# Reordering the loads and set-up between the layer passes and the spectral mixing of a Fourier tokenizer kernel

## Chip, cores, metric

One core of one Trainium2 chip (trn2) runs the whole program once. The metric is the device time of that execution in microseconds (us). TensorE, VectorE, ScalarE, GpSimd and SyncE are called PE, DVE, ACT, POOL and SP, as in the profile. SP issues all the DMA transfers.

## What is computed

128 images of 64 x 64 x 3 go through a tokenizer of four Fourier layers with 32 channels, then through a small head (three dense layers), and the 64 x 64 result of each image is the token input of a transformer block (scan, attention, experts). The change lies in the tokenizer alone:

```python
h = layer_norm(x @ fc0_w + fc0_b, ln0_g, ln0_b)
for i in range(4):
    x1 = spectral_conv(h, w1[i], w2[i])   # rfft2, mix channels on 12 + 12 x 12 modes, irfft2
    x2 = einsum('bchw,oc->bohw', h, conv_w[i]) + conv_b[i]
    h = layer_norm(x1 + x2, ln_g[i], ln_b[i])
    if i < 3: h = gelu(h)
h = gelu(h @ fc1_w + fc1_b); h = gelu(h @ fc2_w + fc2_b); h = h @ fc3_w + fc3_b
```

## The kernel before

**Passes and mixings.** The images are worked in 64 pairs. A pass runs over all pairs, two per loop turn (`halves` = 32 turns); the parity of a pair is p, and most buffers are doubled by p. The first pass lifts the pixels and normalizes them; for each pair it stores the activation (`act_scratch`, 1024 KB, st_a) and its forward spectrum (`spectrum_in`, two DMAs of 78 KB, st_x). A mixing follows: for each of 12 ky it loads the spectrum of all images (`x_in`, 832 KB) and a block of weights (`w_raw`, 208 KB), multiplies them, and stores the result (`spectrum_out`, 832 KB, y_out). The next pass loads for each pair the activation (`act_in`) and the mixed spectrum (`z_in`, two DMAs), adds the pointwise convolution and the inverse transform in the banks H[0..3], normalizes and transforms forward again. So the order is: first pass, mixing 1, pass, mixing 2, pass, mixing 3, pass, mixing 4, last pass (with the head), and then the transformer block. Each engine runs its own hand-written stream, and semaphores order them. There are four passages into a mixing and four out of one.

**SP** (`layer_body`, L1187 to L1197): it issues the two weight blocks of ky 0 and 1 (L1190), waits for the last activation, runs `sp_layer` (L1059: conv_w, conv_b, then four times gain and shift, each a DMA with one value per partition, then gain_row and shift_row, 12 DMAs in all; some of them stand behind waits for the last stores), then `mix` (x_in of ky 0 and 1, then for each ky: w_raw and x_in of the ky two further on, and the store of this one). After the last stores have landed (y_out) it issues act_in and the two z_in of pairs 0 and 1 (`sp_load`, L243).

**DVE** (`body`, L1297): `dve_layer` (L1077) waits for all DMAs of sp_layer, copies conv_w four times (L1079), spreads the bias (L1081), takes the centred conv_w from PE (L1083) and builds conv_block (L1085). Before the last layer it also scales fc1. Then `dve_center` subtracts the mean from a weight block (L1041, L1044; w_cen) and `dve_mix` copies four combined banks into w_mix (L1055). In `two_ky` the order is centre of ky+1, copies of ky, centre of ky+2, copies of ky+1, so a weight block that is late holds back the copies behind it.

**PE** (`body`, L1217): it waits for the ends of the pass, then `pe_layer` (L1091, a product in bank TP), before the last layer a small product for fc1 (L1227), `pe_combine` of ky 0 (L978, four products of 416 columns into COMBINED = TC, TP, M[0], M[1]), then `pe_mix`: transposes of x_in into H[0], H[1] (L992), copied by ACT (L1023), products with w_mix into H[2], H[3] (L1005), copied by ACT to y_sb (L1032). The combination of the next ky is issued after the second of the four groups. f32 products show up as two matmul records each.

**Next pass.** In the three middle passes PE begins with `conv(0)` (L508, needs act_in and all y_sb), then `inverse_x` (L495, needs z_in), conv(1), `inverse_y` (L516). In the last pass it begins with inverse_x (L730), in two halves with an ACT copy between.

Of the kernel before, what the change touches and what calls it, by code (L numbers as in the profile page):

```python
# [101 lines left out]
def build_tokenizer(nc, io, place, h0, debug=None):  # L102
# [3 lines left out]
    with ExitStack() as ctx:  # L106
# [75 lines left out]
        layer_in = sem("layer_in")  # L182
        set_up = sem("set_up")
# [59 lines left out]
        def sp_load(e, P, p, n, first):  # L243
# [6 lines left out]

            at_least(e, h_ready, 8 * P + 4 * p - 4)
# [720 lines left out]
        def pe_combine(e, m, p, layer):  # L972

            q, q0 = 2 * m + p, NY * layer
            e.wait_ge(w_cen_s, q0 + q + 1)
            for s in range(4):
                since(e, w_mix_s, 4 * q0, 4 * (q - 1) + s + 1)
                e.matmul(COMBINED[s][:, 0:NK * C], const("combine")[:, 128 * s:128 * s + 128], w_cen[p][:, :],  # L978
                         start=True, stop=True).then_inc(combined, 1)

        def pe_mix(e, m, p, layer, more):
# [13 lines left out]

            turn(0)
# [51 lines left out]
        def dve_mix(e, m, p, layer):  # L1048

            q, q0 = 2 * m + p, NY * layer  # L1050
            since(e, y_pe, 4 * q0, 4 * (q - 1))
            for s in range(4):
# [3 lines left out]
                              COMBINED[s][:, 0:NK * C].rearrange("r (k g c) -> r k g c", g=8, c=4)).then_inc(w_mix_s, 1)  # L1056


        def sp_layer(e, n, layer, norm):  # L1059

            if layer is not None:
                e.dma_start(conv_raw[:, :], io["conv_w"][layer]).then_inc(layer_in, 16)
                e.dma_start(bias_raw[:, :], io["conv_b"][layer].unsqueeze(1)).then_inc(layer_in, 16)
            g, b = norm
            for u in range(4):
                if layer is not None and u < 2:

                    e.wait_ge(st_a[u], 16 * halves * (layer + 1))
                elif layer is not None:

                    e.wait_ge(st_x[u - 2], 32 * halves * (layer + 1))
                e.dma_start(gain[32 * u:32 * u + 32, :], g.unsqueeze(1)).then_inc(layer_in, 16)
                e.dma_start(shift[32 * u:32 * u + 32, :], b.unsqueeze(1)).then_inc(layer_in, 16)
            e.dma_start(gain_row[:, :], g.partition_broadcast(128)).then_inc(layer_in, 16)
            e.dma_start(shift_row[:, :], b.partition_broadcast(128)).then_inc(layer_in, 16)

        def dve_layer(e, n):  # L1077
            e.wait_ge(layer_in, 160 + 192 * (n + 1))
# [4 lines left out]
            e.tensor_copy(conv_col[:, :], TP[:, 0:C]).then_inc(conv_set, 1)  # L1083
# [45 lines left out]
        def _(e):  # L1129
# [13 lines left out]
            sp_layer(e, 0, None, (io["ln0_g"], io["ln0_b"]))  # L1143

            def one_pass(first, last, start):
# [41 lines left out]
            def layer_body(layer, last):  # L1187

                for p in range(2):
                    e.dma_start(w_raw[p][:, :], io["w_mix"][layer, p]).then_inc(w_in[p], 16)  # L1190

                e.wait_ge(act_ready, 8 * halves * (layer + 1))
                sp_layer(e, layer + 1, layer, (io["ln_g"][layer], io["ln_b"][layer]))
# [3 lines left out]
                one_pass(False, last, halves * (layer + 1))  # L1197
# [9 lines left out]
        def _(e):  # L1207
# [9 lines left out]
            def body(layer, last):  # L1217
                e.wait_ge(h_ready, 8 * halves * (layer + 1))

                e.wait_ge(unit_ready, 8 * halves * (layer + 1))  # L1220
                e.wait_ge(act_ready, 8 * halves * (layer + 1))
                e.wait_ge(f2_ready, 2 * halves * (layer + 1))
                pe_layer(e, layer)
                if last:
                    e.wait_ge(param_in, 16 * 13)
                    e.wait_ge(layer_in, 160 + 192 * LAYERS)
                    e.matmul(TC[:, 0:1], fc1_rep[0:C, :], shift[0:C, 0:1], start=True, stop=True).then_inc(fold_pe, 1)  # L1227
                    e.wait_ge(fold_set, 2)
                pe_combine(e, 0, 0, layer)
# [1112 lines left out]
```

## Time and profile before

| what | us |
|---|---|
| median of 3 runs (lowest, highest) | 7504.2 (7502.06, 7505.27) |
| the profiled execution | 7507.06 |
| its span | 7505.3 |
| busy in the span: PE, PEld, DVE, ACT, POOL | 6631.2, 4040.7, 4763.8, 4363.1, 4229.2 |
| mean granted clock of PE | 0.941 of full |

The first pass ends at about 777 us; the mixings run from 777 to 900, 1849 to 1970, 2920 to 3042 and 3995 to 4119 us; the last pass runs to about 5800 us. The rest is the transformer block. The granted clock is 1.00 at 2.4 GHz and 0.50 at 1.2 GHz. In the timeline a row gives the start, the length, engine, line and operation, and in brackets how long the engine was idle before it and what ended that.

### The profile page before, as it was taken

The numbers are of one execution on the slowest core, as the hardware profiler recorded it, in microseconds if no ns is written. First come the engines' busy times: TensorE is split into PE (matmuls) and PEld (weight loads), VectorE is DVE, ScalarE is ACT, GpSimd is POOL, SyncE is SP. The second block draws the span as 40 slices with busy tenths as digits, with TensorE's granted clock in tenths as the row PEclk, the third lists the DMA queues.
The fourth block names the chain that finished last, engine by engine and source line by source line (L and its number), as shares of the span: only waits on it lengthen the run. The fifth ranks groups of instructions, "written<-read, shape, count | busy, mean of one in ns | idle before, by whom it ended". The sixth has DMA issues, their size and how long they took to land. (4 is left out here: it accounts for less than half of the span.)

```text
span 7505.3 us, 138420 instructions
## 1 busy us (share of the span) xinstructions
PE 6631.2 (88%) x43634; PEld 4040.7 (54%) x43634; DVE 4763.8 (63%) x7329; ACT 4363.1 (58%) x8209; POOL 4229.2 (56%) x1540
## 2 busy tenths in 40 slices
PE   8999799998899998999997999999996577777778
PEld 3444566665666665666665444444443355555455
DVE  8999477776577775577774333333333777777774
ACT  5666466765566665566664677777775233333332
POOL 8999277776377774577771444444444423333320
PEclk9999899999999999999998999999998688888888
DMA  2333455554555554455554111111112333223330
GB/s 97 112 112 116 165 167 167 167 167 142 187 167 167 166 165 162 166 167 167 167 165 171 47 46 53 46 52 47 47 52 60 97 73 72 54 55 72 72 72 3
DMA packets 597031, 835.04 MB, mean 111 GB/s; under 512 B 451945, under 2 KB 493033, under 8 KB 531305
## 3 DMA queue, kind: packets, MB, share of 16 engines
q1 hardware_dynamic: 596968, 834.27, 35.7%
q8 instruction: 32, 0.52, 0.0%
q14 instruction: 31, 0.25, 0.0%
HBM read 477.54 MB, written 356.58 MB: 111 GB/s over the span
## 5 line engine op out<-in xcount | busy, mean ns | idle before, releaser
L949 POOL TENSOR_TENSOR sb_rstd<-sb_var,sb_minus_half 128x16 f32<-128x16 f32 x1280 | 3692.0, 2901 | 2046.8 <-DVE sb_var L900 1017.2
L691 DVE TENSOR_TENSOR sb_unit<-H,sb_rstd 128x512 f32<-128x512 f32 x768 | 528.8, 689 | 685.4 <-POOL sb_rstd L949 547.5
L508 PE MATMUL H<-sb_conv_block,sb_act_in 128*128 128x128 f32 x6144 | 827.2, 283 | 35.1 <-DMA sb_act_in<-act_scratch 28.3
L508 PEld LDWEIGHTS H<-sb_conv_block,sb_act_in 128*128 128x128 f32 x6144 | 732.7, 192 | 150.6 <-issue 141.4
L613 ACT ACTIVATE sb_act_px<-sb_unit 128x512 f32<-128x512 f32 x768 | 483.9, 630 | 496.5 <-DVE sb_unit L697 496.5
L912 DVE COPY sb_act_out<-TC 128x512 f32<-128x512 f32 x256 | 177.0, 691 | 595.3 <-PE TC L758 595.3
L636 ACT ACTIVATE sb_act_out<-TC 128x512 f32<-128x512 f32 x768 | 448.4, 584 | 182.0 <-PE TC L523 182.0
L775 PE MATMUL M<-sb_dense,sb_fc_w 128*64 128x512 f32 x2048 | 521.5, 608 | 30.7 <-ACT sb_dense L858 25.5
L694 DVE TENSOR_TENSOR sb_unit<-sb_unit,sb_gain_row 128x512 f32<-128x512 f32 x768 | 531.2, 692 | 26.2
L697 DVE TENSOR_TENSOR sb_unit<-sb_unit,sb_shift_row 128x512 f32<-128x512 f32 x768 | 531.2, 692 | 26.1
L684 DVE TENSOR_REDUCE sb_var<-sb_square 128x16 f32<-128x528 f32 x768 | 501.0, 693 | 72.8 <-ACT sb_square L606 72.8
L523 PE MATMUL TC<-sb_table,sb_act_px 128*128 128x128 f32 x3072 | 485.2, 281 | 61.6 <-ACT sb_act_out L636 61.2
L537 PE MATMUL TP<-sb_act_px,sb_table 128*52 128x256 f32 x3072 | 496.5, 402 | 0.0
L858 ACT ACTIVATE sb_dense<-M,sb_fc_shifted 128x512 f32<-128x512 f32 x512 | 324.4, 684 | 291.1 <-PE H L767 291.1
L606 ACT ACTIVATE sb_square<-H 128x512 f32<-128x512 f32 x768 | 417.4, 600 | 96.7 <-PE H L516 96.7
L523 PEld LDWEIGHTS TC<-sb_table,sb_act_px 128*128 128x128 f32 x3072 | 333.6, 142 | 255.3 <-ACT sb_act_px L613 215.9
L1972 ACT ACTIVATE blk_silu<-bank 114x260 f32<-114x260 f32 x384 | 148.8, 388 | 551.9 <-PE bank L1705 550.3
L2289 POOL TENSOR_TENSOR blk_rows_b<-blk_rows_b,blk_rows_bb 128x1040 f32<-128x1040 f32 x64 | 176.8, 2763 | 464.7 <-DVE blk_rows_b L2071 464.4
L516 PE MATMUL H<-sb_v_sb,sb_table 52*128 52x512 f32 x1536 | 434.1, 642 | 0.0
L495 PEld LDWEIGHTS M<-sb_table,sb_z_in 96*52 96x52 f32 x6144 | 359.7, 128 | 113.5 <-issue 82.2
L495 PE MATMUL M<-sb_table,sb_z_in 96*52 96x128 f32 x6144 | 407.3, 275 | 0.0
L864 ACT ACTIVATE sb_dense<-M,sb_fc_bias 128x512 f32<-128x512 f32 x512 | 352.3, 688 | 84.7 <-PE M L775 60.3
(276 smaller groups left out, 13123.9 us busy)
## 6 DMA issues: line engine op xcount, KB each, us to landing
act_scratch<-sb_act_out SPq DMA_DIRECT2D x256, 1024.0 KB, 3.9
sb_act_in<-act_scratch SPq DMA_DIRECT2D x256, 1024.0 KB, 5.3
spectrum_in<-sb_f_sb SPq DMA_DIRECT2D x512, 78.0 KB, 1.8
sb_x_in<-spectrum_in SPq DMA_DIRECT2D x48, 832.0 KB, 4.3
spectrum_out<-sb_y_sb SPq DMA_DIRECT2D x48, 832.0 KB, 4.6
sb_z_in<-spectrum_out SPq DMA_DIRECT2D x512, 78.0 KB, 5.0
blk_rows_b<-scan_rows SPq DMA_DIRECT2D x128, 260.0 KB, 6.8
blk_rows_bb<-scan_rows SPq DMA_DIRECT2D x128, 260.0 KB, 7.7
```

Of the source, the lines that this page charges most:

```text
L495: mm = e.matmul(M[u][64 * t:64 * t + 52, 128 * g:128 * g + 128], z, gb[:, t], start=True, stop=True, skip_group_check=True)
L508: e.matmul(H[j][:, 128 * u:128 * u + 128], act_in[p][:, 128 * b:128 * b + 128], conv_block[:, :], start=(u == 0), stop=False, skip_group_c ...
L523: mm = e.transpose(TC[:, 128 * u:128 * u + 128], act_px[k % 2][:, 128 * u:128 * u + 128], const("ident"))
L537: mm = e.matmul(dst, const("f1"), src[:, :, 16 * h:16 * h + 16], start=True, stop=True, skip_group_check=True)
L613: e.activation(act_px[k % 2][:, :], unit[k % 2][:, :], gelu).then_inc(px_ready, 1)
L636: e.activation(act_out[q][:, 512 * k:512 * k + 512], TC[:, :], ACT.Copy).then_inc(act_ready, 1)
L684: e.tensor_reduce(var[j][:, :], square[j % 2][:, :].rearrange("p (y c) -> p y c", c=C + 1), AX.X, ALU.add).then_inc(var_ready, 1)
L691: e.tensor_tensor(rows, H[k][:, :].rearrange("p (y c) -> p y c", c=C), rstd[k][:, :].unsqueeze(2).to_broadcast([128, 16, C]), ALU.mult).th ...
L694: e.tensor_tensor(rows, rows, gain_row[:, :].unsqueeze(1).to_broadcast([128, 16, C]), ALU.mult).then_inc(scaled, 1)
L697: e.tensor_tensor(rows, rows, shift_row[:, :].unsqueeze(1).to_broadcast([128, 16, C]), ALU.add).then_inc(affine_ready, 1)
L775: mm = e.matmul(FC1[w][64 * v:64 * v + 64, :], fc2_w[:, :], dense1[2 * w + v][:, :], start=True, stop=True, skip_group_check=True)
L949: e.tensor_tensor(rstd[j][:, :], var[j][:, :], minus_half[:, :], ALU.pow).then_inc(rstd_ready, 1)
```

## The change

- `sp_layer` is taken apart. `sp_rows` issues gain_row and shift_row. `sp_conv` issues conv_w, conv_b and the weight blocks of ky 0 and 1, with a semaphore of their own (conv_in), for the coming layer: at the start of the kernel for layer 0, and for the others in the pass before, behind its first z_in loads. The column forms of gain and shift, read only before the last pass, are loaded once, at the start.
- At the passage in, SP waits for the last spectrum stores, issues x_in of ky 0 and 1, then the two rows, then act_in of pairs 0 and 1 of the next pass, then the loop of the mixing. At the passage out, it issues only z_in of pairs 0 and 1 (and `sp_conv` behind them).
- `dve_layer` waits for conv_in alone. `pe_layer` uses H[0] in place of TP and waits for unit_ready alone. ky 0 is combined into H[0..3] ahead of PE's waits for act_ready and f2_ready. As the transposes of ky 0 write H[0], they wait until DVE has copied all four banks. DVE centres ky 0 ahead of the fc1 step.

```diff
+        def sp_load_act(e, P, p, n):
             at_least(e, h_ready, 8 * P + 4 * p - 4)
             e.dma_start(act_in[p][:, :], act_d[n]).then_inc(ld[p], 16)
+        def sp_load_spectrum(e, p, n):
             for i in range(2):
                 e.dma_start(z_in[p] ...).then_inc(zl[p], 16)
...
         def pe_combine(e, m, p, layer):
+            banks = H if isinstance(m, int) and q == 0 else COMBINED
...
         def pe_mix(e, m, p, layer, more):
+            if zero:
+                e.wait_ge(w_mix_s, 4 * q0 + 4)
             turn(0)
...
+        def sp_rows(e, norm):
             g, b = norm
             e.dma_start(gain_row[:, :], g.partition_broadcast(128)).then_inc(layer_in, 16)
             e.dma_start(shift_row[:, :], b.partition_broadcast(128)).then_inc(layer_in, 16)
+        def sp_conv(e, layer):
+            e.dma_start(conv_raw[:, :], io["conv_w"][layer]).then_inc(conv_in, 16)
+            e.dma_start(bias_raw[:, :], io["conv_b"][layer].unsqueeze(1)).then_inc(conv_in, 16)
+            for p in range(2):
+                e.dma_start(w_raw[p][:, :], io["w_mix"][layer, p]).then_inc(w_in[p], 16)
         def dve_layer(e, n):
-            e.wait_ge(layer_in, 160 + 192 * (n + 1))
+            e.wait_ge(conv_in, 32 * (n + 1))
...
         def pe_layer(e, n):
             e.wait_ge(conv_set, 4 * n + 2)
-            e.matmul(TP[:, 0:C], conv_rep[:, :], const("center"), start=True, stop=True).then_inc(conv_pe, 1)
+            e.matmul(H[0][:, 0:C], conv_rep[:, :], const("center"), start=True, stop=True).then_inc(conv_pe, 1)
...
@@ SP, start @@
-            sp_layer(e, 0, None, (io["ln0_g"], io["ln0_b"]))
+            for u in range(4):
+                e.dma_start(gain[32 * u:32 * u + 32, :], io["ln_g"][LAYERS - 1].unsqueeze(1)).then_inc(param_in, 16)
+                e.dma_start(shift[32 * u:32 * u + 32, :], io["ln_b"][LAYERS - 1].unsqueeze(1)).then_inc(param_in, 16)
+            sp_rows(e, (io["ln0_g"], io["ln0_b"]))
+            sp_conv(e, 0)
...
@@ SP, one_pass @@
                     for p in range(2):
-                        sp_load(e, base, p, p, False)
+                        sp_load_spectrum(e, p, p)
+                    if not last:
+                        sp_conv(e, layer + 1)
...
@@ SP, mix @@
-                for p in range(2):
-                    sp_mix_load(e, 0, p, layer)
...
@@ SP, layer_body @@
                 for p in range(2):
-                    e.dma_start(w_raw[p][:, :], io["w_mix"][layer, p]).then_inc(w_in[p], 16)
+                    e.wait_ge(st_x[p], 32 * halves * (layer + 1))
+                for p in range(2):
+                    sp_mix_load(e, 0, p, layer)
                 e.wait_ge(act_ready, 8 * halves * (layer + 1))
-                sp_layer(e, layer + 1, layer, (io["ln_g"][layer], io["ln_b"][layer]))
+                sp_rows(e, (io["ln_g"][layer], io["ln_b"][layer]))
+                for p in range(2):
+                    e.wait_ge(st_a[p], 16 * halves * (layer + 1))
+                    sp_load_act(e, halves * (layer + 1), p, p)
                 mix(layer)
...
@@ PE, body @@
-                e.wait_ge(h_ready, 8 * halves * (layer + 1))
                 e.wait_ge(unit_ready, 8 * halves * (layer + 1))
+                pe_layer(e, layer)
+                pe_combine(e, 0, 0, layer)
                 e.wait_ge(act_ready, 8 * halves * (layer + 1))
                 e.wait_ge(f2_ready, 2 * halves * (layer + 1))
-                pe_layer(e, layer)
...
@@ DVE, body @@
                 dve_layer(e, layer)
+                dve_center(e, 0, 0, layer)
                 if last:
...
-                dve_center(e, 0, 0, layer)
                 two_ky(0, True)
...
+                e.wait_ge(layer_in, 32 * (layer + 2))
```

## Rows read from the trace of the kernel before

**Rows 1.** waits view: who waited for whom, us in total, times, longest:

```profile
...
DVE sb_conv_rep L1079 <- DMA sb_shift_row<-in_ln_b_dram: 77.5, 4, 19.9
...
PE TP L1091 <- DVE sb_bias_cols L1081: 48.0, 4, 12.4
```

**Rows 2.** timeline, first passage into mixing: start us, us, engine line op, x count, [idle before]:

```profile
...
774.66 1.63 PE L343 MATMUL M<-sb_f_sb,sb_table 128*48 128x416 f32 x4 [0.61 <-ACT sb_f_sb L394]
...
776.88 0.78 SPq L264 DMA_DIRECT2D spectrum_in<-sb_f_sb  x2
...
785.14 0.90 SPq L963 DMA_DIRECT2D sb_x_in<-spectrum_in  x2
...
788.70 0.63 PE L1091 MATMUL TP<-sb_table,sb_conv_rep 32*128 32x32 f32 x2 [12.41 <-DVE sb_bias_cols L1081]
...
791.07 1.75 PE L978 MATMUL TC<-sb_w_cen,sb_table 128*128 128x416 f32 x2 [1.73 <-DVE sb_w_cen L1044]
...
796.66 1.08 PE L992 MATMUL H<-sb_table,sb_x_in 128*128 128x128 f32 x8
...
796.86 0.88 DVE L1055 COPY sb_w_mix<-M 128x416 f32<-128x416 f32 x1 [0.37 <-PE M L978]
...
798.04 0.48 PE L1005 MATMUL H<-sb_w_mix,sb_x_t 128*128 128x128 f32 x2 [0.30 <-ACT sb_x_t L1023]
```

**Rows 3.** timeline, later ky of the first mixing:

```profile
...
806.47 1.13 PE L1005 MATMUL H<-sb_w_mix,sb_x_t 128*128 128x128 f32 x8 [0.43 <-ACT sb_x_t L1023]
806.63 0.34 SPq L961 DMA_DIRECT2D sb_w_raw<-in_w_mix_dram  x1
...
811.05 0.59 DVE L1041 TENSOR_REDUCE sb_w_sum<-sb_w_raw 128x13 f32<-128x416 f32 x1 [6.24 <-DMA sb_w_raw<-in_w_mix_dram]
...
815.36 1.16 PE L1005 MATMUL H<-sb_w_mix,sb_x_t 128*128 128x128 f32 x8 [1.49 <-DVE sb_w_mix L1055]
...
824.89 1.16 PE L1005 MATMUL H<-sb_w_mix,sb_x_t 128*128 128x128 f32 x8 [2.09 <-DVE sb_w_mix L1055]
```

**Rows 4.** timeline, first passage out of mixing:

```profile
...
899.57 0.35 SPq L252 DMA_DIRECT2D sb_act_in<-act_scratch  x1
899.96 1.38 SPq L254 DMA_DIRECT2D sb_z_in<-spectrum_out  x2
...
906.80 3.10 PE L495 MATMUL M<-sb_table,sb_z_in 96*52 96x128 f32 x32
...
910.91 1.13 PE L516 MATMUL H<-sb_v_sb,sb_table 52*128 52x512 f32 x4
```

**Rows 5.** timeline, fourth passage out of mixing:

```profile
...
4119.20 1.32 SPq L254 DMA_DIRECT2D sb_z_in<-spectrum_out  x2
...
4125.14 1.95 PE L730 MATMUL H<-sb_table,sb_z_in 96*52 96x128 f32 x16 [10.29 <-DMA sb_z_in<-spectrum_out]
```

**Rows 6.** page, DMA issues (count, KB each, us to landing):

```profile
...
spectrum_in<-sb_f_sb SPq DMA_DIRECT2D x512, 78.0 KB, 1.8
...
sb_z_in<-spectrum_out SPq DMA_DIRECT2D x512, 78.0 KB, 5.0
```

**Rows 7.** tile sb_x_in, 776 to 800 us: landing of its two loads, from issue:

```profile
...
DMA to landing us min/median/max: 5.3/6.1/6.8
```

**Rows 8.** timeline, fourth passage into mixing, engine PE:

```profile
...
4005.74 0.60 PE L1091 MATMUL TP<-sb_table,sb_conv_rep 32*128 32x32 f32 x2 [11.34 <-DVE sb_bias_cols L1081]
...
4008.99 1.72 PE L978 MATMUL TC<-sb_w_cen,sb_table 128*128 128x416 f32 x2 [1.46 <-DVE sb_w_cen L1044]
...
4014.60 0.49 PE L1005 MATMUL H<-sb_w_mix,sb_x_t 128*128 128x128 f32 x2 [0.22 <-ACT sb_x_t L1023]
```

**Rows 9.** window: us, busy PE, PEld, DVE, ACT, POOL, granted clock, DMA share, GB/s:

```profile
...
788.00:792.00 4.00, 1.56 (x4) 1.08 (x5) 2.94 (x8) 0.00 (x0) 0.00 (x0) 0.50 0.91 366
```

**Rows 10.** timeline, start of the kernel:

```profile
...
15.68 4.03 SPq L248 DMA_DIRECT2D sb_image_in<-in_x_dram  x3
```

**Rows 11.** window of half a microsecond, columns as in rows 9:

```profile
...
796.50:797.00 0.50, 0.50 (x5) 0.34 (x4) 0.14 (x1) 0.00 (x0) 0.00 (x0) 0.97 0.00 0
```

More of the change, by code:

```diff
@@ L182, in build_tokenizer @@
         layer_in = sem("layer_in")
+        conv_in = sem("conv_in")
         set_up = sem("set_up")
@@ L249, in sp_load @@
                 return
+            sp_load_act(e, P, p, n)
+            sp_load_spectrum(e, p, n)
+        def sp_load_act(e, P, p, n):
             at_least(e, h_ready, 8 * P + 4 * p - 4)
             e.dma_start(act_in[p][:, :], act_d[n]).then_inc(ld[p], 16)
+        def sp_load_spectrum(e, p, n):
             for i in range(2):
@@ L1050, in dve_mix @@
             q, q0 = 2 * m + p, NY * layer
+            banks = H if isinstance(m, int) and q == 0 else COMBINED
             since(e, y_pe, 4 * q0, 4 * (q - 1))
@@ L1055, in dve_mix @@
                 e.tensor_copy(w_mix[p][:, :].rearrange("r (k b c g a) -> r k b g c a", k=NK, b=2, c=4, g=8)[:, :, b, :, :, a],
[L1056 to L1063, printed above, removed]
-            g, b = norm
[L1065 to L1073, printed above, removed]
+                              banks[s][:, 0:NK * C].rearrange("r (k g c) -> r k g c", g=8, c=4)).then_inc(w_mix_s, 1)
+        def sp_rows(e, norm):
+            g, b = norm
             e.dma_start(gain_row[:, :], g.partition_broadcast(128)).then_inc(layer_in, 16)
             e.dma_start(shift_row[:, :], b.partition_broadcast(128)).then_inc(layer_in, 16)
+        def sp_conv(e, layer):
[3 more added lines that the diff above has]
+                e.dma_start(w_raw[p][:, :], io["w_mix"][layer, p]).then_inc(w_in[p], 16)
         def dve_layer(e, n):
-            e.wait_ge(layer_in, 160 + 192 * (n + 1))
+            e.wait_ge(conv_in, 32 * (n + 1))
             e.tensor_copy(conv_rep[:, :].rearrange("o (g c) -> o g c", g=4),
@@ L1082, in dve_layer @@
             e.wait_ge(conv_pe, n + 1)
-            e.tensor_copy(conv_col[:, :], TP[:, 0:C]).then_inc(conv_set, 1)
+            e.tensor_copy(conv_col[:, :], H[0][:, 0:C]).then_inc(conv_set, 1)
             e.wait_ge(conv_set, 4 * n + 3)
@@ L1142, in _, with one_pass @@
             e.dma_start(fc3_bias[:, :], io["fc3_b"].partition_broadcast(128)).then_inc(param_in, 16)
-            sp_layer(e, 0, None, (io["ln0_g"], io["ln0_b"]))
-            def one_pass(first, last, start):
+            for u in range(4):
[3 more added lines that the diff above has]
+            sp_conv(e, 0)
+            def one_pass(first, last, start, layer=None):
                 base = start
@@ L1196, in layer_body @@
                     e.wait_ge(y_out[p], 16 * (NY // 2) * (layer + 1))
-                one_pass(False, last, halves * (layer + 1))
+                one_pass(False, last, halves * (layer + 1), layer)
             one_pass(True, False, 0)
@@ L1217, in body @@
             def body(layer, last):
-                e.wait_ge(h_ready, 8 * halves * (layer + 1))
                 e.wait_ge(unit_ready, 8 * halves * (layer + 1))
+                pe_layer(e, layer)
+                pe_combine(e, 0, 0, layer)
                 e.wait_ge(act_ready, 8 * halves * (layer + 1))
                 e.wait_ge(f2_ready, 2 * halves * (layer + 1))
-                pe_layer(e, layer)
                 if last:
-                    e.wait_ge(param_in, 16 * 13)
-                    e.wait_ge(layer_in, 160 + 192 * LAYERS)
+                    e.wait_ge(param_in, 16 * 21)
                     e.matmul(TC[:, 0:1], fc1_rep[0:C, :], shift[0:C, 0:1], start=True, stop=True).then_inc(fold_pe, 1)
                     e.wait_ge(fold_set, 2)
-                pe_combine(e, 0, 0, layer)
                 for p in range(2):
@@ L1259, in body @@
                         act_mix(e, m, p, layer)
-                e.wait_ge(layer_in, 160 + 192 * (layer + 1))
                 if last:
-                    e.wait_ge(param_in, 16 * 13)
+                    e.wait_ge(param_in, 16 * 21)
                     e.wait_ge(fold_set, 2)
@@ L1293, in _ @@
                             fc0_rep[:, :].unsqueeze(1).to_broadcast([97, 32, C]), ALU.mult).then_inc(set_up, 1)
-            e.wait_ge(layer_in, 160)
+            e.wait_ge(layer_in, 32)
             first_pass(fori, lambda *at: dve_first(e, *at))
```

5 lines of the change are left out of this document (2 added, 3 removed).

## The prediction

> **What bounds the kernel now.** I read the waits view first, then the timeline at one passage into a mixing, the mixing behind it and one passage out, and looked whether the others repeat them. The waits view has two entries that come just four times each: DVE's first copy of a layer waits 77.5 us in all, ended by the last DMA of `sp_layer`, and PE's first product behind it waits 48.0 us, 12.4 at most [rows 1]. The timeline of the first passage shows what stands there [rows 2]. PE's last product of the pass ends at 774.66 + 1.63 = 776.29. SP stores the spectrum, issues its string of small DMAs, and only when the last has landed does DVE begin, so L1091 starts at 788.70. Then come the centring, four combining products at half clock, four copies, and the first product of the mixing at 798.04. So a passage in costs 21.7 us, with PE idle for more than half of it.
>
> Inside the mixing the beat, from one ky's L1005 to the next, is 8.43, then 8.89 and 9.53 us [rows 3]. What ends the longer ones is a weight block that lands late: w_raw is issued at 806.63, DVE gets it at 811.05, and L1005 of the next ky starts 4.31 us behind that, at 815.36. At the passage out SP issues act_in at 899.57 and the two z_in from 899.96; PE starts the inverse transform at 906.80 [rows 4]. In the last passage out z_in itself releases PE, at 4125.14 [rows 5].
>
> The change touches these eight places and the start, and nothing of the passes, where I expect the same time.
>
> **The sum, passages in.** (1) conv_w, conv_b and the first weight blocks are now there, so L1091 may follow PE's last product at once. That is the whole idle of [rows 1]: 48.0 us for four. (2) From L1091 to the first combination it stays 791.07 - 788.70 = 2.37 us, and from there to the end of the copies 797.74 - 791.07 = 6.67: at the first passage 778.7 and 785.35. (3) The transposes of ky 0 lay under the combination and now stand behind the copies, as they share H. From L992 to L1005 are 1.38 us [rows 2]; so far L1005 followed the copies by 0.30. With 0.07 for the signal that is 1.15 lost each time, 4.6 in all; L1005 comes at 786.8. (4) x_in must be there by 785.35. The second of the spectrum stores is issued at about 777.25 and lands 1.8 later [rows 2, 6], so x_in is issued at 779.2 and lands 5.3 later [rows 7], at 784.5: 0.9 us to spare, and a later one would be paid in full. (5) Before the last layer the fc1 step goes from between: 4008.99 - 4005.74 = 3.25 against 2.37, a gain of 0.9 [rows 8]. (6) In that passage the clock had risen earlier (5.61 us from L978 to L1005 against 6.97 in the first) [rows 2, 8]; I give back half of that, 0.7.
>
> (7) A new debt: SP has put two act_in behind the two x_in, before the weight block of ky 2. From the issue of the two x_in, 785.14 and some 0.45 behind it, to the later landing (6.8 from its issue) are 7.2 us [rows 2, 7]. Of these their 1.70 MB take 4.2, as 366 GB/s over a DMA share of 0.91 is about 402 at full share [rows 9]. The other 3.0 are latency. With 3.80 MB and the 0.5 of the weights ky 2's block lands at 779.2 + 3.0 + 9.5 + 0.5 = 792.2. DVE centres it ahead of the copies of ky 1: 1.2 for the centring and 3.3 for the copies give L1005 of ky 1 at 796.8 where the beat asked for 786.8 + 8.43 = 795.2. The block of ky 3 is issued when ky 0's store is, some 8.6 us behind ky 0's L1005, so at 795.4; it lands 4.4 later, at 799.8, and L1005 of ky 2 could come at 804.1. It can't come sooner than about 8 us behind ky 1's, 804.8. Of the debt of 1.6 about 0.7 stays, 2.8 in all. This rests on order: one x_in lands behind the other [rows 7], and I let the weights wait for all that is issued before them. The Trainium skill, DMA: Bandwidth & Descriptors, section "Queues, rings and completion order", has each engine take one issuer's descriptors in ring order, though a later write may end first. If the block went past the activations it would be there at 786.4 by the 4.4 us of [rows 3], and the debt would be nothing: the sum would be 2.8 larger.
>
> Passages in: 48.0 - 4.6 + 0.9 - 0.7 - 2.8 = 40.8 us.
>
> **Passages out.** act_in is there, so conv(0) runs right behind the mixing. The two z_in are issued from 899.57, the second at 900.26. In the last passage the second was issued at 4119.86 and PE went at 4125.14, 5.3 later [rows 5] (the median is 5.0 [rows 6]), with a 1 MB act_in before it that takes 2.6 at 402 GB/s. Without it 2.7, so at 902.95, 3.85 before 906.80. Ends: as short as the store of the same 78 KB, 1.8, and as long as now, 5.3. I take the middle, since the 1 MB is certainly gone and pieces this small are not. PE now idles between conv(0) and z_in, so both inverses run at half clock: 16 products take 1.95 there [rows 5], 3.9 for 32 against 3.10, and conv(1) may stay slow; against 4.11 up to L516 [rows 4] I count 5.1. 2.8 us stay. In the last passage the clock is half either way and 0.4 + 2.6 = 3.0 go; I take 2.8 too. Four: 11.2 us. By the Trainium skill (same page, section "Anatomy of one DMA", a fit for the other DMA path) a transfer takes 2.0 us and its bytes at 436 GB/s, so 2.2 for z_in: 2 us more in all.
>
> **Start.** Four more DMAs stand before the images: 0.39 to 0.45 us of issue each [rows 2, 4], and 0.43 MB of weights take 1.1 us of the queues partly before the images do. Nothing hides it, since every engine's first work comes from the images, issued so far at 15.68 [rows 10]: 2.0 us lost (1.6 to 2.8).
>
> At no cost: `sp_conv` inside a pass, four issues of some 0.4 us behind z_in, while SP waits for the first pair's H anyway, past 910.91 in the first passage out [rows 4]; without that cover 3 x 1.6. The removal of eight small DMAs a passage is part of (1).
>
> **Sum:** 40.8 + 11.2 - 2.0 = 50.0 us. The profiled execution took 7507.06 (span 7505.3), so 7457.1; the median of the runs is 2.9 lower: **7454.2**.
>
> **Rivals.**
> - *The weights of ky 2 are later and stay late* (0.28). If they land 1.2 us later still (0.9 for 366 GB/s in place of 402, 0.3 for the two row DMAs between) and the later beats give nothing back, each passage in keeps 806.47 - 798.0 = 8.5: 34 for four. If z_in also lands no sooner than now, the passages out bring 1 in all (three times 906.80 - 905.56 - 1.0, and 0.4), else 11. Less the 2 of the start the gain is 33 to 43: 7461 to 7471. For it: DVE's fixed order. Against: the third ky's block isn't delayed.
> - *The clock is back sooner* (0.12). PE works up to 776.9 in place of idling, so the four combinations may run at full clock. They take 5.6 us, from 791.07 to 796.66, and the clock rises only as they end [rows 2, 11]; at full clock DVE's copies would set 4.4 in place of 6.67, so up to 2.3 a passage, 9 in all: 7445. Against: the clock of ky 0 matters little if ky 2's weights hold the second beat.
> - *The beat of the mixings grows* (0.06), the slower end. Two act_in start each mixing out of step, and beats lock on the long form, 9.53 in place of 8.43: 1.1 us for 44 beats is 48 [rows 3], which eats the gain (no change); from 1.5 us a beat on (66) it ends at 7520, slower. Each has 0.03. Against: the long beats come from the distance of store and weights, which the change leaves.
> - *It gains little* (0.04): x_in, not the string of small DMAs, proves to hold the mixing, as the spectrum's landing can't be moved. Were x_in 6 us later than in (4), 24 go: 7478.
>
> The forecast has 0.50. The range holds the first two rivals' times and the bounds: 7438 to 7472. The runs before spread 3.2 us, and 0.2% (15 us) is about what can be told from no change. Faster by more than that 0.94, within 0.03, slower 0.03.
>
> **What would show it.** L1079 right behind DVE's last work of the pass and L1091 right behind the last product; L978 2.4 us later; L1005 of ky 0 about 1.4 behind the last copy; DVE idle before ky 2's L1041, ended by w_raw, at about 792; L508 of a middle pass at once behind the mixing, and L495 3.4 us behind the first z_in; the first image load issued at about 17.5. It is wrong if L1079 still waits on a DMA, if L992 of ky 0 waits for x_in, or if the beats from ky 3 on differ by more than 0.2 us.

## The result and the profile after

The changed kernel takes 7468.2 us (median of 4 runs, 7464.8 to 7470.9) against 7504.7 (4 runs): ratio 0.9952, with a 95% interval of 0.9937 to 0.9967. That is 36.6 us less, where 50 were forecast and 7438 to 7472 was the range. The profiled execution took 7464.83 (span 7463.0), the fastest of the four, so the two profiles differ by 42.3 us, six more than the medians.

To see where they went I cut both timelines at the same four marks of each layer: the start of the pass's last product (L343, L559; now L352, L568), the first product of ky 0 and of ky 11 (L1005, now L1017), and the first inverse_y (L516, L751; now L525, L760). All times are differences of row starts, in us.

| stretch | before | after | difference |
|---|---|---|---|
| start to the first pass's last product | 774.7 | 776.3 | +1.6 |
| passages in, 1 to 4 | 23.4, 23.0, 23.3, 21.8 | 11.6, 12.0, 12.2, 15.8 | -39.9 |
| mixings, ky 0 to ky 11 | 93.5, 92.3, 92.6, 96.4 | 99.5, 95.9, 94.4, 95.3 | +10.2 |
| passages out, ky 11 to inverse_y | 19.3, 19.9, 21.0, 21.5 | 17.5, 17.4, 17.0, 20.9 | -9.0 |
| three middle passes | 2809.7 | 2807.0 | -2.7 |
| last pass and the block | 3372.8 | 3370.3 | -2.5 |

The last two rows hold no edit. Over these two kernels and all the runs below they go from 2807.0 (the changed kernel itself, the lowest) to 2810.9 and from 3369.6 to 3373.8, so their 5.2 us are within what the same work varies by from run to run. The other four rows make 37.1 us, close to the 36.6 of the medians.

The timeline of the first passage and its mixing, answering to [rows 2, 3]:

```profile
...
776.30 1.63 PE L352 MATMUL M<-sb_f_sb,sb_table 128*48 128x416 f32 x4 [0.61 <-ACT sb_f_sb L403]
...
777.86 0.63 PE L1099 MATMUL H<-sb_table,sb_conv_rep 32*128 32x32 f32 x2
...
780.22 5.33 PE L988 MATMUL H<-sb_w_cen,sb_table 128*128 128x416 f32 x8 [1.73 <-DVE sb_w_cen L1056]
...
780.86 0.84 SPq L972 DMA_DIRECT2D sb_x_in<-spectrum_in  x2
...
783.21 0.92 SPq L258 DMA_DIRECT2D sb_act_in<-act_scratch  x2
...
784.64 0.34 SPq L970 DMA_DIRECT2D sb_w_raw<-in_w_mix_dram  x1
...
787.92 0.49 PE L1017 MATMUL H<-sb_w_mix,sb_x_t 128*128 128x128 f32 x2 [0.22 <-ACT sb_x_t L1035]
...
794.92 0.59 DVE L1053 TENSOR_REDUCE sb_w_sum<-sb_w_raw 128x13 f32<-128x416 f32 x1 [8.48 <-DMA sb_w_raw<-in_w_mix_dram]
...
799.05 2.07 PE L1017 MATMUL H<-sb_w_mix,sb_x_t 128*128 128x128 f32 x8 [3.13 <-DVE sb_w_mix L1068]
```

L1099 follows the last product at once, L988 comes 2.36 us later, and the first product of ky 0 at 787.92, 11.6 us behind the start of L352. Then comes the debt: two act_in of 1 MB are issued at 783.21, the weights of ky 2 at 784.64, and DVE gets these only at 794.92. Ky 1's product starts at 799.05, 11.1 us behind ky 0's where 8.43 were so before. The tile view of w_raw, 783 to 800 us, has the landing of its two loads (from issue, min, median, max):

```profile
...
DMA to landing us min/median/max: 4.5/7.4/10.3
```

The long one is ky 2's. What follows the wait costs too. Two windows of the same stretch (busy PE, PEld, DVE, ACT, POOL, granted clock, DMA share, GB/s):

```profile
...
797.00:798.00 1.00, 0.00 (x0) 0.00 (x0) 1.00 (x2) 0.00 (x0) 0.00 (x0) 1.00 0.97 406
...
799.00:800.00 1.00, 0.95 (x4) 0.96 (x5) 0.00 (x0) 0.00 (x0) 0.00 (x0) 0.50 0.96 394
```

PE stood idle from 796, the clock fell to half, and the eight records (four products) at 799.05 took 2.07 us, where the same eight took 1.13 [rows 3].

The fourth passage in, timeline, answering to [rows 8]:

```profile
...
3964.55 0.28 DVE L1313 TENSOR_SCALAR sb_fc_scaled<-sb_fc_rep,sb_gain 128x128 f32<-128x128 f32 x1
...
3964.78 5.36 PE L988 MATMUL H<-sb_w_cen,sb_table 128*128 128x416 f32 x8 [1.83 <-DVE sb_w_cen L1056]
...
3970.06 0.38 PE L1241 MATMUL TC<-sb_shift,sb_fc_rep 32*128 32x1 f32 x2
3970.48 0.16 DVE L1315 TENSOR_TENSOR sb_fc_shifted<-TC,sb_fc_bias 128x1 f32<-128x1 f32 x1 [5.65 <-PE TC L1241]
...
3971.67 2.93 DVE L1068 COPY sb_w_mix<-H 128x416 f32<-128x416 f32 x4
...
3974.75 1.95 PE L1002 MATMUL H<-sb_table,sb_x_in 128*128 128x128 f32 x8 [4.31 <-DVE sb_w_mix L1068]
...
3979.11 0.59 DVE L1053 TENSOR_REDUCE sb_w_sum<-sb_w_raw 128x13 f32<-128x416 f32 x1 [4.51 <-DMA sb_w_raw<-in_w_mix_dram]
...
3979.31 1.06 PE L1002 MATMUL H<-sb_table,sb_x_in 128*128 128x128 f32 x4
...
3987.85 1.16 PE L1017 MATMUL H<-sb_w_mix,sb_x_t 128*128 128x128 f32 x8 [0.26 <-ACT sb_x_t L1035]
```

DVE has issued L1313 at 3964.55 and then waits for L1241, which PE takes only behind all four combinations. So the copies of ky 0 begin at 3971.67, when they could have begun 1.8 us into the combination. PE idles 4.3 us ahead of L1002, and at 3979.31 it is still at half clock (four transposes in 1.06 us, 0.61 at full clock). Ky 1's product comes at 3987.85, 11.3 us behind ky 0's. The weights of ky 2 are there at 3979.11, in the midst of ky 0, and what releases the product is ACT, so this long beat is one at half clock and not one of late weights.

The first passage out, timeline, answering to [rows 4]:

```profile
...
891.90 1.15 PE L517 MATMUL H<-sb_conv_block,sb_act_in 128*128 128x128 f32 x8 [0.67 <-ACT sb_y_sb L1044]
895.26 2.77 SPq L263 DMA_DIRECT2D sb_z_in<-spectrum_out  x4
...
899.64 3.66 PE L504 MATMUL M<-sb_table,sb_z_in 96*52 96x128 f32 x32 [6.59 <-DMA sb_z_in<-spectrum_out]
...
904.82 1.13 PE L525 MATMUL H<-sb_v_sb,sb_table 52*128 52x512 f32 x4
```

conv(0) runs behind the mixing, and L504 starts 4.4 us behind the first z_in, all of it at half clock (3.66; the 3.10 of [rows 4] were at half clock too up to 909.2, where the grant rose). The start, answering to [rows 10], and two entries of the waits view, of which the second is no loss (DVE is early now) and the first has grown from 159.8 us before:

```profile
...
17.49 4.06 SPq L249 DMA_DIRECT2D sb_image_in<-in_x_dram  x3
```

```profile
...
DVE sb_w_sum L1053 <- DMA sb_w_raw<-in_w_mix_dram: 182.3, 40, 8.5
...
DVE sb_conv_col L1091 <- PE H L1099: 32.5, 4, 8.4
```

### The profile page after: what moved, and what is told of

Its sections match the earlier page's. It is cut to its first block and busy times, and to the rows that moved or that the text cites. A ratio compares the mean times of both kernels' runs of the same rounds, so it can differ in the third digit from the quotient of the medians.

```text
span 7463.0 us, 138376 instructions
## 1 busy us (share of the span) xinstructions
PE 6635.4 (89%) x43634; PEld 4046.9 (54%) x43634; DVE 4764.8 (64%) x7329; ACT 4360.1 (58%) x8209; POOL 4226.9 (57%) x1540
## 5 line engine op out<-in xcount | busy, mean ns | idle before, releaser
L615 ACT ACTIVATE sb_square<-H 128x512 f32<-128x512 f32 x768 | 417.0, 600 | 96.4 <-PE H L525 96.2
L525 PE MATMUL H<-sb_v_sb,sb_table 52*128 52x512 f32 x1536 | 433.7, 641 | 0.0
L504 PEld LDWEIGHTS M<-sb_table,sb_z_in 96*52 96x52 f32 x6144 | 359.8, 128 | 132.8 <-issue 101.5
L504 PE MATMUL M<-sb_table,sb_z_in 96*52 96x128 f32 x6144 | 407.5, 275 | 19.4 <-DMA sb_z_in<-spectrum_out 19.4
```

Of the source, the lines that this page charges most:

```text
L504: mm = e.matmul(M[u][64 * t:64 * t + 52, 128 * g:128 * g + 128], z, gb[:, t], start=True, stop=True, skip_group_check=True)
```

## The experiments

Each kernel was run beside the kernel before and profiled, and the table has the same stretches as above (sums over the layers). The kernel before came to 7502.2 to 7504.7 in these comparisons. For a difference of less than some 20 us between two of the kernels below the 95% intervals of their ratios to before (16 to 25 us wide) overlap; what is read from such a difference rests on runs whose ranges lie apart and on the stretches of the profiles.

| kernel | median (range) | passages in | of these the fourth | mixings | passages out |
|---|---|---|---|---|---|
| before | 7504.7 | 91.5 | 21.8 | 374.8 | 81.8 |
| changed | 7468.2 (7464.8 to 7470.9) | 51.6 | 15.8 | 385.0 | 72.8 |
| after_again | 7467.6 (7466.8 to 7468.2) | 50.4 | 16.2 | 385.5 | 72.2 |
| act_late | 7456.6 (7453.7 to 7458.4) | 51.0 | 15.1 | 374.6 | 72.6 |
| act_out | 7471.4 (7469.3 to 7478.8) | 48.3 | 15.1 | 375.3 | 89.3 |
| ky0_combined | 7466.9 (7465.5 to 7471.1) | 46.4 | 14.1 | 390.9 | 72.1 |
| late_fold | 7451.7 (7443.9 to 7454.1) | 45.3 | 11.3 | 374.1 | 71.6 |
| late_comb_fold | 7446.8 (7445.5 to 7448.5) | 43.3 | 11.4 | 372.9 | 72.6 |
| w_early | 7439.9 (7436.8 to 7441.1) | 51.1 | 16.1 | 359.5 | 73.1 |
| all_parts | 7427.3 (7426.9 to 7429.0) | 42.9 | 10.8 | 354.5 | 72.0 |
| conv_wait_only | 7483.3 (7477.1 to 7491.4) | 72.8 | 21.4 | 375.2 | 82.8 |
| x_behind | 7475.9 (7474.8 to 7477.8) | 66.4 | 16.2 | 380.1 | 71.0 |

**after_again.** The changed kernel with no edit.

> The changed kernel unaltered, to see what repeats. In its profile the mixings (first product of ky 0 to first product of ky 11, 11 beats) took 99.5, 95.9, 94.4 and 95.3 us against 93.5, 92.3, 92.6 and 96.4 before. If the longer beats belong to the change, the first mixing comes out at 97 us or more again and the sum of the four at 382 to 388. If they were chance, the sum falls to about 375, as before, and the time with it by 10 us.

The mixings took 99.2, 94.3, 95.0 and 97.0 us, 385.5 in all, and the time was 7467.6. The 10 us repeat, so they belong to the change.

**act_late.**

```diff
-                for p in range(2):
-                    e.wait_ge(st_a[p], 16 * halves * (layer + 1))
-                    sp_load_act(e, halves * (layer + 1), p, p)
                 mix(layer)
...
                         sp_mix_store(e, m, p, layer)
+                for p in range(2):
+                    e.wait_ge(st_a[p], 16 * halves * (layer + 1))
+                    sp_load_act(e, halves * (layer + 1), p, p)
                 for p in range(2):
                     sp_mix_store(e, NY // 2 - 1, p, layer)
```

> The two act_in of the coming pass are issued behind the loop of the mixing, ahead of its last two stores, in place of ahead of ky 2's weight block. Theory (the activations hold up ky 2's weights, and the beats behind them run out of step): ky 2's L1053 no longer waits long for w_raw, the first beat is 8.4 in place of 10.4 to 11.3 us, the four mixings take 374 to 378 us in place of 385, conv(0) still runs right behind the mixing, and the time falls by 7 to 10 us. Rival (the beats are long because x_in and the stores collide in a mixing that begins earlier): first beat still over 10 us and no gain. Second rival (the activations collide with the last stores): mixings short, but y_out lands up to 5 us later at each passage out, gain eaten.

The mixings are back at 374.6 (the first two are 6.5 and 3.6 us shorter than in the changed kernel, the third and fourth 0.2 or less), the passages out keep their gain, and the time falls by 11 us to 7456.6 (no run above 7458.4, where the changed kernel had none below 7464.8), ratio to before 0.9937 (0.9920 to 0.9953). The timeline of the first mixing:

```profile
...
783.64 0.33 SPq L970 DMA_DIRECT2D sb_w_raw<-in_w_mix_dram  x1
...
788.18 0.49 PE L1017 MATMUL H<-sb_w_mix,sb_x_t 128*128 128x128 f32 x2 [0.22 <-ACT sb_x_t L1035]
788.45 0.59 DVE L1053 TENSOR_REDUCE sb_w_sum<-sb_w_raw 128x13 f32<-128x416 f32 x1 [1.73 <-DMA sb_w_raw<-in_w_mix_dram]
...
796.65 1.13 PE L1017 MATMUL H<-sb_w_mix,sb_x_t 128*128 128x128 f32 x8 [0.47 <-ACT sb_x_t L1035]
```

The block is issued at 783.64 and lands 4.8 us later, and ky 1's product comes 8.47 behind ky 0's. So neither rival holds. One thing came otherwise: the third mixing's first beat was 10.1 us and the fourth's 11.0. The fourth is the one at half clock from above, with ky 2's weights not in the way here either. In the third DVE had ky 2's weights before the first product of ky 0; its windows have the clock:

```profile
...
2902.00:2904.00 2.00, 1.25 (x9) 1.06 (x9) 0.75 (x2) 0.70 (x2) 0.00 (x0) 1.00 0.40 127
2904.00:2906.00 2.00, 2.00 (x10) 1.81 (x11) 0.91 (x2) 0.38 (x1) 0.00 (x0) 0.73 0.00 0
2906.00:2908.00 2.00, 2.00 (x12) 2.00 (x11) 0.00 (x0) 1.26 (x2) 0.00 (x0) 0.50 0.00 0
```

PE had begun this ky at full clock and was granted half in the midst of it.

**act_out.** The same lines behind the four z_in of `one_pass`.

> The two act_in of the coming pass are issued at the passage out, behind the four z_in. This undoes the part of the change that loads the activations ahead. Theory: mixings as short as in act_late (374 to 378 us in all), z_in landing as in the changed kernel, but conv(0) waits for act_in, 4 to 6 us later than z_in, so each passage out of the first three loses 2 to 4 us against the changed kernel; in total within 4 us of the changed kernel. Rival (the early activations are what the passages out gain by): passages out as long as before the change, 19.3 to 21.5 us from ky 11 to inverse_y, and the time 9 us more in these, against 10 less in the mixings.

The mixings were short again (375.3), but the passages out took 89.3 us, longer than before the change (81.8) and outside what either side expected. PE's timeline:

```profile
...
898.85 2.07 PE L517 MATMUL H<-sb_conv_block,sb_act_in 128*128 128x128 f32 x8 [13.45 <-DMA sb_act_in<-act_scratch]
900.85 3.66 PE L504 MATMUL M<-sb_table,sb_z_in 96*52 96x128 f32 x32
...
906.45 2.08 PE L525 MATMUL H<-sb_v_sb,sb_table 52*128 52x512 f32 x4
```

act_in lands 6.3 us after its issue, behind four transfers of small pieces, and releases PE at 898.85, 13.45 us after its last work. So loading the activations ahead is worth 16.5 us at the passages out (89.3 - 72.8) against issuing them behind z_in, and 9.0 against the order before, where they led z_in; it costs 9.7 in the mixings (385.0 - 375.3) where it stands in the change.

**ky0_combined.** In this kernel the fc1 product before the last layer writes over one column of TC, a combined bank, before its copy, so that column of the last layer's ky 0 weights isn't computed.

```diff
-            banks = H if isinstance(m, int) and q == 0 else COMBINED
+            banks = COMBINED
...
-            if zero:
-                e.wait_ge(w_mix_s, 4 * q0 + 4)
...
                 pe_layer(e, layer)
-                pe_combine(e, 0, 0, layer)
                 e.wait_ge(act_ready, 8 * halves * (layer + 1))
                 e.wait_ge(f2_ready, 2 * halves * (layer + 1))
+                pe_combine(e, 0, 0, layer)
```

The first of these edits stands in `dve_mix` too.

> ky 0 is combined in TC, TP, M0 and M1 again, behind the waits for act_ready and f2_ready, and the first transposes no longer wait for the four copies. Theory (the move to the pixel banks buys nothing, since the spectrum copy ends 1.7 us before the weights are centred, and costs 1.2 us): the combination starts at the same distance from the pass's last product, 3.9 us, and ky 0's first product follows the last copy by 0.3 in place of 1.4, if x_in is there; x_in lands about as the copies end, so the gain is 0.3 to 1.2 us in each of the first three passages, 1 to 4 us in all. Rival (f2_ready or act_ready does hold PE): the combination starts over 0.3 us later and the kernel is slower by 1 to 3 us.

The combination starts 3.92 to 4.01 us behind the last product's start, the very distance of the changed kernel, so f2_ready held nothing. The passages in are 5.1 us shorter and the time is the same, as the mixings took it back:

```profile
...
785.71 0.48 PE L1015 MATMUL H<-sb_w_mix,sb_x_t 128*128 128x128 f32 x2 [0.30 <-ACT sb_x_t L1033]
...
793.79 0.59 DVE L1051 TENSOR_REDUCE sb_w_sum<-sb_w_raw 128x13 f32<-128x416 f32 x1 [8.59 <-DMA sb_w_raw<-in_w_mix_dram]
...
797.90 2.07 PE L1015 MATMUL H<-sb_w_mix,sb_x_t 128*128 128x128 f32 x8 [4.18 <-DVE sb_w_mix L1066]
```

Counted from the last product (775.10 here), ky 0 begins 1.0 us earlier than in the changed kernel and the weights of ky 2 don't, so ky 1 waits for them: its beat is 12.2 us.

**late_fold.** act_late and, in PE's `body`:

```diff
                 e.wait_ge(unit_ready, 8 * halves * (layer + 1))
+                if last:
+                    e.wait_ge(act_ready, 8 * halves * (layer + 1))
+                    e.wait_ge(param_in, 16 * 21)
+                    e.matmul(TC[:, 0:1], fc1_rep[0:C, :], shift[0:C, 0:1], start=True, stop=True).then_inc(fold_pe, 1)
                 pe_layer(e, layer)
...
                 if last:
-                    e.wait_ge(param_in, 16 * 21)
-                    e.matmul(TC[:, 0:1], fc1_rep[0:C, :], shift[0:C, 0:1], start=True, stop=True).then_inc(fold_pe, 1)
                     e.wait_ge(fold_set, 2)
```

> act_late and, before the last layer, the small fc1 product ahead of conv_w's product, so that DVE's fc1 step doesn't wait behind the four combinations. Theory (in the fourth passage the four copies of ky 0 start only when all four combinations and the fc1 product are done, since DVE waits for the product ahead of its copies): from the pass's last product to ky 0's first product 11.5 to 12.5 us in place of 15.1 to 15.8 in the fourth passage, PE no longer idle for 4.3 us before its first transposes, and the first beat of the fourth mixing 8.3 in place of 11 us, because the clock isn't lost. Gain against act_late 3 to 6 us. Rival (the fourth passage is long for its clock alone): unchanged within 1 us.

The fourth passage takes 11.3 us in place of 15.1, and its first beat 8.27 in place of 11.0:

```profile
...
3963.88 1.17 PE L1002 MATMUL H<-sb_table,sb_x_in 128*128 128x128 f32 x8 [1.03 <-DVE sb_w_mix L1068]
...
3965.27 0.49 PE L1017 MATMUL H<-sb_w_mix,sb_x_t 128*128 128x128 f32 x2 [0.22 <-ACT sb_x_t L1035]
...
3973.54 1.16 PE L1017 MATMUL H<-sb_w_mix,sb_x_t 128*128 128x128 f32 x8 [0.27 <-ACT sb_x_t L1035]
```

In the median 4.9 us are gained against act_late, though one run of four was as low as 7443.9. So the long first beat of the fourth mixing, too, came from the fc1 step.

**late_comb_fold.** late_fold and the edit of ky0_combined, with the fc1 product in H[1].

> late_fold with ky 0 combined in TC, TP, M0 and M1 as before the change (the fc1 product goes to H1). In ky0_combined the passages in became 5 us shorter and the mixings 5 us longer, since ky 2's weights held ky 1 at its place. Theory (with the weights no longer held up the 1.2 us of each passage is a gain): passages in 10.6 to 11.0 us in place of 11.7 to 12.2, mixings 92 to 95 each, 3 to 5 us less than late_fold. Rival (x_in is what holds ky 0, and the combination hid behind it): passages as long as in late_fold.

4.9 us less than late_fold in the median, and no overlap with it but for that one run. The passages in come to 10.5, 10.9, 10.7 and 11.4 against 11.0, 12.0, 11.0 and 11.3. The profile shows 2 of the 4.9 there; the rest lies within what such stretches vary by, so it isn't shown to be a gain.

**w_early.** act_late, and in `mix` each block of weights one step earlier:

```diff
+                sp_mix_load_w(e, 1, 0, layer)
-                with fori(0, NY // 2 - 1) as m:
-                    for p in range(2):
-                        sp_mix_load(e, m + 1, p, layer)
-                        sp_mix_store(e, m, p, layer)
+                with fori(0, NY // 2 - 2) as m:
+                    sp_mix_load_x(e, m + 1, 0, layer)
+                    sp_mix_load_w(e, m + 1, 1, layer)
+                    sp_mix_store(e, m, 0, layer)
+                    sp_mix_load_x(e, m + 1, 1, layer)
+                    sp_mix_load_w(e, m + 2, 0, layer)
+                    sp_mix_store(e, m, 1, layer)
```

(sp_mix_load is split in its two halves; the last turn is written out.)

> act_late with each weight block issued a step earlier: ahead of the store of a ky in place of behind it. Theory (the beat of 8.4 to 9 us is set by DVE waiting for a weight block that SP issues only when a store is ready; without that wait it is the 7.98 us seen where the weights are there): DVE's waits for w_raw fall from 160 to 180 us in all to under 60, beats of 7.98 throughout but the first, mixings 88 to 90 us in place of 92 to 95, gain 14 to 20 us against act_late. Rival (the mixing is held by the transfers as such, 832 KB in, 832 KB out and 208 KB of weights a ky): the weights wait in the queue instead, beats as before.

16.7 us less than act_late. The beats behind the first are 7.7 to 8.3, the mixings 89.0 to 90.8. But DVE's wait for weights fell only from 161.9 to 142.9 us, not under 60:

```profile
...
810.54 0.33 SPq L976 DMA_DIRECT2D sb_w_raw<-in_w_mix_dram  x1
...
812.28 1.13 PE L1026 MATMUL H<-sb_w_mix,sb_x_t 128*128 128x128 f32 x8 [0.54 <-ACT sb_x_t L1044]
...
814.86 0.59 DVE L1062 TENSOR_REDUCE sb_w_sum<-sb_w_raw 128x13 f32<-128x416 f32 x1 [3.50 <-DMA sb_w_raw<-in_w_mix_dram]
...
820.55 1.13 PE L1026 MATMUL H<-sb_w_mix,sb_x_t 128*128 128x128 f32 x8 [0.54 <-ACT sb_x_t L1044]
```

DVE still waits 3.5 us for the block at 814.86, but that is now while PE works on the groups before, and what releases L1026 at 812.28 and 820.55 is ACT. In the waits views of act_late and of w_early, PE's products wait like this:

```profile
...
PE H L1017 <- DVE sb_w_mix L1068: 31.4, 33, 1.8
```

```profile
...
PE H L1026 <- ACT sb_x_t L1044: 23.5, 47, 0.6
```

In w_early no product waited for w_mix. The length of DVE's wait says nothing here; what counts is whether it ends last.

**all_parts.** act_late, the fc1 product ahead, ky 0 in COMBINED, weights a step earlier, and `sp_conv(0)` behind the first three image loads.

> act_late, the fc1 product ahead, ky 0 in TC, TP, M0, M1, weights a step earlier, and at the start conv_w, conv_b and the two weight blocks behind the first three image loads. Each part's theory holds: start 1.6 us shorter (last product of the first pass at 774.7), passages in 10.6 to 11.2 each, mixings 88 to 90, passages out 17 to 17.5 (the fourth 20.5): about 7427 to 7435 us. If the beat is held by transfers, 7448.

7427.3 us, ratio 0.9898 (0.9882 to 0.9915) to before. The start is 2.8 us shorter than in the changed kernel (773.5), where 1.6 were expected; the first pass alone varies by some 1 us (774.7 in the kernel before and 773.4 in conv_wait_only, which have the same start).

**conv_wait_only.** The kernel before, with:

```diff
-                e.dma_start(conv_raw[:, :], io["conv_w"][layer]).then_inc(layer_in, 16)
-                e.dma_start(bias_raw[:, :], io["conv_b"][layer].unsqueeze(1)).then_inc(layer_in, 16)
+                e.dma_start(conv_raw[:, :], io["conv_w"][layer]).then_inc(conv_in, 16)
+                e.dma_start(bias_raw[:, :], io["conv_b"][layer].unsqueeze(1)).then_inc(conv_in, 16)
...
         def dve_layer(e, n):
-            e.wait_ge(layer_in, 160 + 192 * (n + 1))
+            e.wait_ge(conv_in, 32 * (n + 1))
...
                 if last:
                     e.wait_ge(param_in, 16 * 13)
+                    e.wait_ge(layer_in, 160 + 160 * LAYERS)
```

The other waits for layer_in count 160 a layer in place of 192.

> The kernel before with one part alone: conv_w and conv_b count on a semaphore of their own, and DVE's first copy waits for these two, not for the ten small DMAs behind them. Nothing is issued earlier, and x_in still stands behind all of them. Theory (the string of DMAs held the passage through one wait and through x_in's place in SP's queue): DVE starts about 6 us earlier, the combination ends before x_in lands, and x_in, issued some 10.5 us behind the pass's last product and landing 5.3 later, becomes the holder: from the last product to ky 0's first product 17 to 18 us in place of 23, so 20 to 24 us less in all. Rival (the wait for the small DMAs is the whole of it): 11 to 13 us in a passage, as in the changed kernel. Second rival (x_in or the weights hold it anyway): within 2 us of 23.

The first three passages took 17.2, 16.9 and 17.2 us, as the theory had it. x_in ends last:

```profile
...
781.10 0.63 PE L1092 MATMUL TP<-sb_table,sb_conv_rep 32*128 32x32 f32 x2 [6.04 <-DVE sb_bias_cols L1082]
...
783.46 1.75 PE L979 MATMUL TC<-sb_w_cen,sb_table 128*128 128x416 f32 x2 [1.73 <-DVE sb_w_cen L1045]
...
784.04 0.90 SPq L964 DMA_DIRECT2D sb_x_in<-spectrum_in  x2
...
789.16 1.19 PE L993 MATMUL H<-sb_table,sb_x_in 128*128 128x128 f32 x8 [0.47 <-DMA sb_x_in<-spectrum_in]
...
790.65 0.48 PE L1006 MATMUL H<-sb_w_mix,sb_x_t 128*128 128x128 f32 x2 [0.30 <-ACT sb_x_t L1024]
```

But it does so by 0.47 us only. The combination itself starts 10.0 us behind the pass's last product (773.43), where the changed kernel has 3.9, since conv_w and conv_b are still issued behind the pass. So of the 40 us at the passages in, 19 come from the one wait; the other 21 need the loads of conv_w and conv_b ahead of the passage and x_in first, and no run has the one without the other. The fourth gained just 0.4, since its fc1 step still waits for the last small DMA.

**x_behind.** The changed kernel, with:

```diff
-                for p in range(2):
-                    e.wait_ge(st_x[p], 32 * halves * (layer + 1))
-                for p in range(2):
-                    sp_mix_load(e, 0, p, layer)
                 e.wait_ge(act_ready, 8 * halves * (layer + 1))
                 sp_rows(e, (io["ln_g"][layer], io["ln_b"][layer]))
                 for p in range(2):
                     e.wait_ge(st_a[p], 16 * halves * (layer + 1))
                     sp_load_act(e, halves * (layer + 1), p, p)
+                for p in range(2):
+                    e.wait_ge(st_x[p], 32 * halves * (layer + 1))
+                for p in range(2):
+                    sp_mix_load(e, 0, p, layer)
```

> The changed kernel with x_in of ky 0 and 1, and the waits for the spectrum stores, behind the two rows and the two act_in, so the spectrum's loads no longer lead. Theory (in the changed kernel ky 1 is held by ky 2's weights, which come last in either order, so what ky 0 loses its first beat gives back): passages in 3 to 5 us longer each, first beats 3 to 5 us shorter, and the time within 3 us of the changed kernel. Rival (what ky 0 loses is lost): 12 to 18 us slower than the changed kernel.

Both missed: the kernel is 8 us slower than the changed one. The first three passages in are 4.6 to 5.1 us longer each, as the theory had it, but the first beats aren't shorter (10.8, 10.5, 11.0, 10.4 against 11.1, 10.5, 10.4, 11.3):

```profile
...
791.38 1.97 PE L1002 MATMUL H<-sb_table,sb_x_in 128*128 128x128 f32 x8 [5.85 <-DMA sb_x_in<-spectrum_in]
...
793.84 0.59 DVE L1053 TENSOR_REDUCE sb_w_sum<-sb_w_raw 128x13 f32<-128x416 f32 x1 [7.42 <-DMA sb_w_raw<-in_w_mix_dram]
...
795.97 1.06 PE L1002 MATMUL H<-sb_table,sb_x_in 128*128 128x128 f32 x4
```

The weights are there at 793.84, in the midst of ky 0. PE had waited 5.85 us for x_in and then ran ky 0 at half clock (four transposes in 1.06 us). So ky 1 was held first by the weights, now by the clock. The mixings were 5 us shorter, most of it behind the first beats, and the passages out 2, which gave 7 of the 15 back.

## Why the prediction was right, and where it was off

The direction and the mechanism held, the sum was 13.4 us too large against the median and 7.7 against the profile, and the time lies in the range, near its end. By its steps:

- **(1) to (4), the wait removed: right.** From the last product's start to the first combination 3.9 us, where (2) had 778.7 - 774.66 = 4.0; ky 0 follows the last copy (786.44) by 1.48, where (3) had 1.45. The first three passages gained 11.8, 11.0 and 11.1, forecast 10.9 to 11.3. x_in was just there, as (4) had it. That the lead of x_in is needed is shown by x_behind, where each of the first three passages lost about 5 us without it.
- **(5), "the fc1 step goes from between": failed.** It went from ahead of the combination to ahead of the copies. I followed DVE's new order only to L1056 and did not ask who is queued behind the wait for fold_pe. The fourth passage gained 6.1 where 10.4 were counted, and the half clock that followed made the mixing's first beat 11.3 in place of 8.3. late_fold gives back 3.8 in the passage and 2.7 in the beat.
- **(7), "Of the debt of 1.6 about 0.7 stays": failed, and is the main miss.** The landing was forecast at 792.2, with the later start of the kernel 793.8, and was 794.9: the transfer was sized nearly right (10.3 us from issue). What I held to be absorbed wasn't. From the pass's last product to ky 1's first product the first three layers gained 9.1, 8.9 and 9.2 us, and the beats from there on gave nothing back (341.7 us over the four mixings, 341.2 before). In all the mixings grew by 10.2 us against the 2.8 of the sum. This is the first rival, "the weights of ky 2 are later and stay late", which let each passage keep 8.5. It had 33 to 43 us and the medians have 36.6; that the profile's 42.3 lie in there as well is luck, since 5.2 of them lie where nothing was edited. act_late shows the cause by taking it away: the first beats of its first two mixings were 8.47 and 8.44 in place of 11.13 and 10.51. The weights are not the whole of it, though. Over what they were before, the four first beats grew by 2.7, 2.1, 1.9 and 3.1; in the third the clock fell as well, as in act_late's (10.1), and the fourth is that of (5): it was 11.0 in act_late and act_out and 8.27 in late_fold. The beats after the first in the first mixing, 9.4, 10.6 and 9.8 (8.89, 9.53 and 8.26 before), may come from stores that ran late behind ky 1, but this isn't shown: act_out, with no activations in the way, had 8.9, 9.6 and 9.9. On the order of the queue, the block landed 10.3 us after its issue, at 794.90, behind both activations (791.57 and 794.40), and 4.8 us after its issue without them (act_late). The Trainium skill, DMA: Bandwidth & Descriptors, section "Queues, rings and completion order", has descriptors taken in ring order, and this trace agrees.
- **Passages out: right in kind, 2.2 too much.** PE waits for the second z_in, which landed 3.5, 3.1, 3.6 and 3.4 us after its issue, where I had 2.7; PE was at half clock as expected. The gains were 1.9, 2.5, 4.0 and 0.6 for 2.8 each. By the Trainium skill, DMA: Bandwidth & Descriptors, section "Anatomy of one DMA", a fit for another DMA path, I had an estimate of 2.2 us for z_in. The traces differ: no z_in at these passages landed under 2.6.
- **Start: 1.6 for 2.0**, the images issued at 17.49 for the 17.5 expected. The mark itself varies by some 1 us, as said under all_parts.
- **The passes: no change**, as forecast.
- **The other rivals did not come.** The clock was not back sooner (granted 0.50 from 776 to 784 us, and the combination took 5.3 us for 5.6), the beats did not lock on a long form (ky 3 to ky 11 took 268.9 us over the four mixings, 267.9 before), and x_in did not hold ky 0. One sign of being wrong did appear by its letter: the beat from ky 3 to ky 4 of the first mixing was 9.84 against 8.26. In after_again it was 8.25.

Not settled: the fall of the clock inside a ky, as in act_late's third mixing, happens in some mixings of a kernel and not in others. It makes 1.6 us a time. Nor is it shown why the median of late_comb_fold is 2.9 us further down than its passages.

## What to carry over

When loads are moved ahead into a gap, look at what is issued behind them on the same queue: here two that nobody needed for 100 us stood before one that was needed in 8, and issuing them late in the stage kept all of their gain and none of the cost (11 us in act_late). When a step is moved on one engine, follow that engine's own order until the next thing another engine waits for. And ask of a wait not how long it is but whether it ends last: DVE waited 143 us for weights in w_early and no product of PE's waited for w_mix; it waited 162 in act_late, and 33 did, for 31 us.

## What the runs showed of the chip

- A 208 KB load landed 2.4 us after issue where only two stores of 78 KB were still under way (the first of the two at the first passage of the kernel before), 4.8 behind two of 832 KB (act_late) and 10.3 behind these and two of 1 MB (the changed kernel).
- In the changed kernel the clock also fell in the midst of a mixing: PE idle from 796, granted 1.00 at 797 and 0.50 at 799, full again past 802. In act_late's third mixing it fell without such an idle stretch: granted 1.00 from 2902 to 2904 and 0.50 from 2906 to 2908, with PE busy 2.00 of the 2 us from 2904 on. By the Trainium skill, TensorE: Matmul & The Clock Gate, section "What's actually happening", the two throttle levels seen are half and full. This trace agrees: where the grant held still it was 0.50 or 1.00.
- A 1 MB load landed 5.0 us after issue at the first passage out of the kernel before, where it led, and 6.3 in act_out, behind four z_in of 78 KB. In the changed kernel the 78 KB of z_in, in pieces of 104 bytes, took 2.7 to 3.5 at that passage, more than the 2.4 of 208 KB of weights.
